# Last layer's state-space stage: the causal mask moves from TensorE to a minimum by VectorE, the weighing moves from VectorE to GpSimd, and the sums of squares are taken one pair later

## The reference, cut to what matters

```python
D_INNER, NHEADS, HEAD_DIM, CHUNK = 4096, 64, 64, 128
zxbcdt = layernorm(x) @ W_in                 # z, x, B, C and dt
xbc = silu(causal_conv1d(xbc, conv_w, conv_b))      # 4 taps
dt = softplus(dt + dt_bias)
dA_cs = cumsum(dt * A)                       # over the 128 tokens
diff = dA_cs[i] - dA_cs[j]
L = exp(where(i >= j, diff, -inf))           # one 128 x 128 matrix for each head and sequence
Y = einsum(C[i], B[j], L[i, j], dt[j] * x[j])
yg = (Y + D * x) * silu(z)
out = (yg * rsqrt(mean(yg * yg) + 1e-5) * norm_w) @ W_out
x = x + out
```

## Time and profile before

| | us |
|---|---|
| median of 3 runs | 1964.93 |
| lowest and highest | 1964.28, 1967.31 |
| the profiled execution, device time | 1967.18 |
| its span, first to last instruction | 1965.4 |
| TensorE busy in the span | 1714.1 (87%) |
| VectorE | 1181.5 (60%) |
| ScalarE | 923.4 (47%) |
| GpSimd | 443.7 (23%) |

### The profile page before, as it was taken

One profiled execution on the slowest core, in us unless ns is written; L12 is line 12 of the kernel. 1 busy time (PEld: TensorE's weight loads), 2 busy tenths in 40 slices (PEclk: granted clock), 3 DMA queues, 4 the chain that ended last, 5 costly groups with the idle time before them and its releaser, 6 DMA issues. The chain is left out here.

```text
span 1965.4 us, 37376 instructions
## 1 busy us (share of the span) xinstructions
PE 1714.1 (87%) x13971; PEld 1340.3 (68%) x13974; DVE 1181.5 (60%) x2340; ACT 923.4 (47%) x1876; POOL 443.7 (23%) x497
## 2 busy tenths in 40 slices
PE   7977746789999899977677879999999997999898
PEld 4766633568999755643467746777777776888666
DVE  3676678555555612225664478888888865666632
ACT  2344466345556512112144256666767654555432
POOL 1020010023333131221300124544545431000200
PEclk9999977899999999998789889999999998999999
DMA  2020000400000182221000000110101103111000
GB/s 98 3 89 3 4 29 9 132 17 25 24 24 24 40 340 38 47 32 61 14 1 3 25 25 18 33 32 24 32 24 32 30 11 120 33 32 32 1 1 22
DMA packets 27104, 77.86 MB, mean 40 GB/s; under 512 B 2928, under 2 KB 14832, under 8 KB 24560
## 3 DMA queue, kind: packets, MB, share of 16 engines
q1 hardware_dynamic: 22912, 71.17, 10.6%
q0 software_dynamic: 4080, 5.13, 1.7%
HBM read 63.01 MB, written 13.28 MB: 39 GB/s over the span
## 5 line engine op out<-in xcount | busy, mean ns | idle before, releaser
L2463 DVE SCALAR_TENSOR_TENSOR arena<-bank,arena 128x508 f32<-128x508 f32 (+2 forms) x204 | 151.5, 743 | 27.6 <-ACT arena L2459 15.6
L217 PE MATMUL bank<-const 128*128 128x256 f32 (+1 forms) x244 | 102.2, 533 | 37.0 <-PEq L65 37.0
L2589 PE MATMUL bank<-L3a_wo,L3a_y_gated 128*128 128x256 f32 x512 | 123.9, 386 | 0.0
L2817 DVE TENSOR_TENSOR L3a_decays<-L3a_decays,L3a_cb_masked 128x512 f32<-128x512 f32 x128 | 94.7, 802 | 43.5 <-ACT L3a_decays L2701 43.5
L2701 ACT ACTIVATE L3a_decays<-bank 128x512 f32<-128x512 f32 x128 | 66.1, 602 | 97.2 <-PE bank L2563 97.2
L2616 PE MATMUL bank<-L3a_xnT_high,L3a_w_high 128*128 128x512 f32 x256 | 105.8, 413 | 1.5 <-ACT L3a_decays L2701 1.5
L2589 PEld LDWEIGHTS bank<-L3a_wo,L3a_y_gated 128*128 128x128 f32 x512 | 92.4, 190 | 17.5 <-issue 7.3
L2616 PE MATMUL bank<-L3a_xnT_high,L3a_w_low 128*128 128x512 f32 x256 | 99.9, 390 | 0.0
L2616 PE MATMUL bank<-L3a_xnT_low,L3a_w_high 128*128 128x512 f32 x256 | 99.7, 389 | 0.0
L217 PEld LDWEIGHTS bank<-const 128*128 128x128 f32 x244 | 44.1, 208 | 63.8 <-issue 63.8
L1879 PE MATMUL bank<-L1f_experts,xnT 128*128 x184 | 84.5, 603 | 2.4 <-DVE xnT L1981 2.4
(11 more groups left out here) (592 smaller groups left out, 4709.0 us busy)
## 6 DMA issues: line engine op xcount, KB each, us to landing
arena<-in_L3p SPq DMA_DIRECT2D x32, 388.0 KB, 3.0
L1f_experts<-in_L1f SPq DMA_DIRECT2D x8, 1536.0 KB, 17.5
arena<-in_L1x SPq DMA_DIRECT2D x18, 384.0 KB, 3.0
arena<-in_L3x SPq DMA_DIRECT2D x18, 384.0 KB, 3.1
arena<-in_L0f SPq DMA_DIRECT2D x1, 4224.0 KB, 13.6
arena<-in_L3f SPq DMA_DIRECT2D x1, 4055.0 KB, 12.3
rows_sent<-L1a_blank SPq DMA_DIRECT2D x1, 2967.0 KB, 12.1
xnT<-rows_sent SPq DMA_DIRECT2D x23, 129.0 KB, 2.0
```

Of the source, the lines that this page charges most:

```text
L217: self.nc.tensor.matmul(self.k.ps[bank][:, 0:width], self.k.ident, self.k.const[:, 0:width], start=True, stop=True)
L2463: return nc.vector.scalar_tensor_tensor(dst[:, :, d:], psum[:, :, 0:P - d], wcol, dst[:, :, d:], ALU.mult, ALU.add)
L2589: mm = nc.tensor.matmul(ps[g // 2][:, (g % 2) * C:(g % 2 + 1) * C], yg[:, o, g * P:(g + 1) * P], wo[:, o, :], start=False, stop=False, ski ...
L2817: nc.vector.tensor_tensor(d, d, cbm[:, 4 * half:4 * half + 4, :].rearrange("p b t -> p (b t)"), ALU.mult).then_inc(S["dec_ready"], 1)
```

## The change

Four things change in this block.

1. TensorE's four mask matmuls of each pair go. In their place VectorE makes once a tile `highest` of 128 x 128 (1e30 where a token may be seen, -1e30 where it may not), and for each pair takes the minimum of the difference bank and `highest` (`bound`), which writes `decays`. The bank is released by VectorE now.
2. ScalarE's exp reads and writes `decays` in SBUF and no longer reads PSUM.
3. The product with `cb_masked` (`weigh`) moves from VectorE to GpSimd, behind a new semaphore `exp_ready`, at the end of GpSimd's pair.
4. `add_squares` moves on GpSimd from the end of pair j, for pair j-2, to the middle of pair j, for pair j-3, behind the split of the weights. Three of them now stand in the tail in place of two.

```diff
-                        nc.tensor.matmul(bank("d", n)[:, :], identr[:, :], later[:, :, :].rearrange("p m t -> p (m t)"),
-                                         start=True, stop=False)
-                    for n in range(4):
                         g = slice(32 * n, 32 * n + 32)
                         nc.tensor.matmul(bank("d", n)[:, :], lrow[g, s, :], rrow[g, :, :].rearrange("p m t -> p (m t)"),
-                                         start=False, stop=True).then_inc(S["diff_psum"], 1)
+                                         start=True, stop=True).then_inc(S["diff_psum"], 1)
...
                 def exponents(act, j, s):
                     for n in range(4):
-                        act.wait_ge(S["diff_psum"], j * 4 + n + 1)
-                        if not early(j):
-                            act.wait_ge(S["y_psum"], j * 2 - 2)
-                        nc.scalar.activation(d4[:, n * HALF:(n + 1) * HALF], bank("d", n)[:, :],
-                                             ACT.Exp).then_inc(S["diff_read"], 1)
+                        act.wait_ge(S["diff_read"], j * 4 + n + 1)
+                        d = d4[:, n * HALF:(n + 1) * HALF]
+                        nc.scalar.activation(d, d, ACT.Exp).then_inc(S["exp_ready"], 1)
...
-                def weigh(dve, j, s):
+                def bound(dve, j, s):
                     for n in range(4):
                         h, half = n // 2, n % 2
-                        d = dec[:, s, h, 4 * half:4 * half + 4, :].rearrange("p b t -> p (b t)")
-                        dve.wait_ge(S["diff_read"], j * 4 + n + 1)
-                        nc.vector.tensor_tensor(
-                            d, d, cbm[:, 4 * half:4 * half + 4, :].rearrange("p b t -> p (b t)"),
-                            ALU.mult).then_inc(S["dec_ready"], 1)
+                        dve.wait_ge(S["diff_psum"], j * 4 + n + 1)
+                        if not early(j):
+                            dve.wait_ge(S["y_psum"], j * 2 - 2)
+                        nc.vector.tensor_tensor(dec[:, s, h, 4 * half:4 * half + 4, :],
+                                                bank("d", n)[:, :].rearrange("p (b t) -> p b t", b=4),
+                                                over(highest[:, :], 4), ALU.min).then_inc(S["diff_read"], 1)
...
+                def weigh(pool, j, s):
+                    if is_first(j):
+                        pool.wait_ge(S["cb_ready"], 2)
+                    for n in range(4):
+                        h, half = n // 2, n % 2
+                        d = dec[:, s, h, 4 * half:4 * half + 4, :].rearrange("p b t -> p (b t)")
+                        pool.wait_ge(S["exp_ready"], j * 4 + n + 1)
+                        nc.gpsimd.tensor_tensor(
+                            d, d, cbm[:, 4 * half:4 * half + 4, :].rearrange("p b t -> p (b t)"),
+                            ALU.mult).then_inc(S["dec_ready"], 1)
...
                     nc.gpsimd.tensor_tensor(wl[:, s, :], w2, wh[:, s, :].bitcast(F32),
                                             ALU.subtract).then_inc(S["w_split"], 1)
+                    if not early(j, 3):
+                        add_squares(pool, j - 3)
...
                         pool.sem_inc(S["slot_read"], 2)
-                    if not early(j):
-                        add_squares(pool, j - 2)
+                    if not is_first(j):
+                        if is_second(j):
+                            weigh(pool, 0, 0)
+                        weigh(pool, j, s)
...
                 def tail(pool):
                     scale_output(pool, N - 1, 1)
-                    add_squares(pool, N - 2)
-                    add_squares(pool, N - 1)
+                    for j in range(N - 3, N):
+                        add_squares(pool, j)
```

More of the change, by code:

```diff
@@ L2432, in l3_attn @@
         ROWS = [[(h, f, r) for h in range(2) for f in range(2) for r in own] for own in ((0, 1), (2, 3))]
-        identr, later = st.sb("ident_r", [P, P], F32R), st.sb("later", [P, 4, P], F32R)
+        highest = st.sb("highest", [P, P])
         lrow = st.sb("diff_left", [P, 2, P], F32R)
@@ L2444, in l3_attn @@
             "bc_ready", "cb_psum", "cb_ready", "da_ready", "z_psum", "x_psum", "z_read", "x_scaled", "x_read",
-            "x_conv", "x_ready", "xt_psum", "xt_read", "diff_psum", "diff_read", "dec_ready",
+            "x_conv", "x_ready", "exp_ready", "xt_psum", "xt_read", "diff_psum", "diff_read", "dec_ready",
             "y_psum", "y_read", "y_ready", "pair_small", "wo_ready", "out_done", "sq_ready", "sq_added",
@@ L2649, in _ @@
                 pe.wait_ge(S["x_low"], 1)
-                pe.wait_ge(S["mask_set"], 2)
                 passes(pe, pair, tail)
@@ L2757, in _ @@
                 nc.vector.memset(zero[:, :], 0.0).then_inc(S["zero_set"], 1)
-                nc.vector.tensor_copy(identr[:, :], k.ident).then_inc(S["mask_set"], 1)
-                nc.vector.tensor_copy(later[:, :, :], over(k.c["causalT"], 4)).then_inc(S["mask_set"], 1)
+                nc.vector.tensor_scalar(highest[:, :], k.c["causalT"], 2.0, BIG, ALU.mult, ALU.add).then_inc(S["mask_set"], 1)
                 dve.wait_ge(S["x_high"], 1)
@@ L2845, in pair @@
                     if not first:
-                        weigh(dve, j, s)
+                        bound(dve, j, s)
                     for half in range(2):
@@ L2868, in pair @@
                     if first:
-                        weigh(dve, j, s)
+                        dve.wait_ge(S["mask_set"], 1)
+                        bound(dve, j, s)
                     else:
```

## The result

The changed kernel takes 1978.59 us, the median of 4 runs (1978.03 to 1979.54). Its ratio to the kernel before (1964.61, the median of 4 runs beside it) is 1.0071 with a 95% interval of 1.0056 to 1.0086: 14 us slower, 11 to 17. The profiled execution has a span of 1977.0 us, 11.6 us more than the 1965.4 before.

The account below looks back on a forecast made before the run. It took TensorE to bound the kernel at 13.69 us a pair, VectorE close behind. Loop 0, collision +8.8, head -4.0 and tail +1.2 gave +6.0 us on 1964.93, so 1971 us, range 1961 to 1980.

Parts of the forecast that it names:

- TensorE's relief is given to the circle: Loop: the masks' 1.22 us a pair leave TensorE but go to a formerly hidden chain; 0, within 2.7 us.
- the circle: VectorE and ScalarE in the loop: minima, last exp, squares, first tap, taps through gate in series; 13.67 us a pair.
- Rival 1: Loop: VectorE's circle is shorter than walked and TensorE's relief comes through, 1929 us at the full 1.22; chance 0.08.
- The products' duration: GpSimd's weighing, 512 elements in two inputs, takes 1.27 us each, judged from additions in place.
- The collision: Every second pair: VectorE's gate waits for GpSimd's addition of squares, 0.65 us with the small copy, 8.8 us in all.
- rival 3: Loop: GpSimd comes later by half a us or more, 1978 us and up; chance 0.17.
- Odd pairs free of it: Before odd pairs GpSimd has no `steps`, is done at 11.4 us, and nothing collides with the gate.
- The exclusion of two-tile operations: A VectorE operation on two SBUF tiles and a GpSimd one exclude each other; bank-and-tile minima and taps do not.
- Head: First pairs: without masks the taps of pair 1 start at 1184.1; -4.0 us, within -2.5 and -5.
- Tail: After the last pairs: three additions of squares with two squares between them before the reduction; +1.2 us.
- The split done by 9.5: GpSimd's split of the weights is done by 9.5 us, TensorE wants it at about 15, so it costs nothing.
- Rival 4: TensorE's idle pieces lower its clock; at 1.2 GHz over 100 us in all; chance 0.01.

Follow-up runs that it names:

- the squares behind the first taps: Changed kernel with ScalarE's squares moved from before the first convolution taps to behind them; 1971.93 us, ratio 1.0041.
- the run behind the gate: Changed kernel, cb_masked and sum of squares moved by 8 bytes, ScalarE's squares ending its pair, GpSimd's addition of squares waiting for VectorE's gate; 1935.33 us, ratio 0.9854.
- The small sum: Changed kernel with GpSimd's addition of squares cut from 1024 to 16 elements per partition; 1964.91 us, ratio 0.9999.
- the wait alone: Changed kernel with GpSimd's addition of squares put behind the copies of dt and D and waiting for the gate, nothing else; 1965.57 us, ratio 0.9999.
- the two tiles moved: Changed kernel with cb_masked moved by 8 bytes and the running sum of squares moved by 8 bytes against the squares; 1964.97 us, ratio 1.0.
- the run with squares at the end: Changed kernel with cb_masked and sum of squares moved by 8 bytes and ScalarE's squares at the very end of its pair; 1990.6 us, ratio 1.013.
- the run with the masks alone: Changed kernel with the weighing left on VectorE, behind the minima, and the squares' sums in their old place; 1967.27 us, ratio 1.0014.

## Why the prediction was right

It gave 1971 us, 1961 to 1980, slower with 0.62; 1978.6 came. That is inside the whole range but outside the 1967 to 1975 of my own forecast, and the loss of 14 us is over twice the 6 that I had summed. The mechanism is the one it named, and its terms stand as follows.

- *TensorE's relief is given to the circle*: predicted 4.77 us from the first minimum to the first tap and 13.67 for the circle; the trace has 4.78 and 13.76. The term, 0 within 2.7 us, measured 14.7 - 12.9 (the collision, below) = 1.8 us. That the circle is the reason is shown by the squares behind the first taps (short pairs 12.9) and by the run behind the gate (12.84, with the squares out of the circle). Rival 1, a circle shorter than TensorE, falls.
- *The products' duration*: predicted 1.27 us from in-place additions, measured 1.30. Right in size, but my reading "in place" was wrong: the place of the tiles decides, 1.09 us with one of them moved. The additions that I took it from and the products are slow for the same reason, so that it came out is in part luck. My estimate of 1.12 us was scaled down from the 4497 ns for 2048 elements that the Trainium skill's page "GPSIMD Engine Reference", section 3.1 Elementwise — side-by-side cycle accounting, gives; the traces have 1.30 and 1.09.
- *The collision*, mis-sized: predicted 0.65 us in every second pair, 8.8 us in all; measured 14.75 - 13.76 = 0.99 us in 13 of the 27, 12.9 us. The walk of GpSimd was short by 0.75 us. `wo` started 0.24 us later (1405.83 - 1404.20 = 1.63 for 1.39): the differences started 0.07 later against the next minimum, behind an output half that ended after `dtx` (below), and they and the second output half took 2.59 for 2.42. Behind `wo` GpSimd paused 0.32 us, where it waits for `wo` itself before it releases the slot; I had not counted it, though the earlier trace rows show 0.26 in the same place. The products took 5.05 us for 4.88. The addition so ended at 13.68 for 12.94. Against that, the gate began 0.12 later, and the small copy did not get between its halves but waited for the first one, 0.45 us for 0.20: the 0.20 us I added for it were nothing. This is the step that failed in size. The time came out as rival 3 had it (GpSimd half a us later, 1978 us), though not from the turn of the loop, which that rival named. TensorE before this long pair, the output halves and the differences between them, where `dtx` ends at 1403.08:

```profile
1401.33 1.89 PE L2586 MATMUL bank<-L3a_wo,L3a_y_gated 128*128 128x256 f32 x8
1403.15 0.67 PE L2560 MATMUL bank<-L3a_diff_right,L3a_diff_left 32*128 32x512 f32 x4
1403.75 1.99 PE L2586 MATMUL bank<-L3a_wo,L3a_y_gated 128*128 128x256 f32 x8
```

- *Odd pairs free of it*: right, 13.76 throughout. The small sum, the wait alone and the two tiles moved each remove the loss of the long pairs and leave the short ones as they are, so it is shown that the collision makes them.
- *The exclusion of two-tile operations*: right. The minima and taps kept their durations beside the products (2.47 and 2.30 us).
- *Head* -4.0, measured -4.4, close by two errors that nearly cancel: the first tap of pair 1 came at 1182.49, not 1184.1, and the gate of pair 3 already met an addition and took 2.41 us, a collision that the sum had only for the loop. (My own steps, 4.5 - 0.7, gave 3.8.) *Tail* +1.2, measured +1.4.
- *The split done by 9.5*: a slip; my own walk has 10.57 before an even pair, and it came later still. Nothing hung on it.
- *The clock*: 1.00 in the loop with TensorE busy 93% of it. Rival 4 falls.

The sum of the terms measured, 14.7 - 4.4 + 1.4 = 11.7 us, is that of the profiled spans. The comparison of runs says 14, between 11 and 17; the rest is not resolved.

## What to carry to other kernels

Taking work off the bound engine gains only as far as the next circle is shorter. Here it was longer than it looked, because exp, squares and first tap, which used to wait side by side with TensorE, became a series; drawing that circle with durations of the trace gave it within 0.1 us. When work goes to GpSimd, ask of each of its instructions which two-tile operation of VectorE it will meet and who waits for that one: the same collision was free with TensorE as the bound, cost 13 us in the changed kernel, and went away by an order that makes GpSimd wait.

## What the runs showed of the hardware

- GpSimd's operation with two different fp32 inputs has two speeds by where the inputs begin. With both at the same place within 16 bytes (both at a multiple, as the products, or both 8 bytes behind one, as the squares) 512 elements took 1.30 us and 1024 took 2.36; with the two 8 bytes apart within 16, 1.09 and 2.00. The bias addition of 256 has 0.72 and 0.63 by the same rule. Only places of 0 and 8 bytes occurred.
- A two-tile operation of VectorE and one of GpSimd exclude each other for whole instructions, and the one that starts later waits. In the run with squares at the end GpSimd's addition started at 1407.82, during the gate's first half, and took 2.31 us in place of 2.00; the second half, from 1408.18, took 2.49 us in place of 0.68. The Trainium skill's page "SBUF — State Buffer", section SBUF: two separate sides, says so, and the durations here agree with it. The same collision the other way is in the run with the masks alone, where GpSimd's addition met VectorE's last two products and took 2.99 us in place of 2.36, while the products kept 0.68 (the last one starts within 0.03 us of the addition, so this run shows the exclusion but not who was first):

```profile
1416.31 2.99 POOL L2919 TENSOR_TENSOR arena<-arena 128x1024 f32<-128x1024 f32 x1 [1.78 <-ACT arena L2702]
```

- ScalarE's exp from SBUF takes 0.63 us, started 0.60 apart behind the minima, against 0.60 from a bank.
